# A graph convolution on one core: longer rows of edges with the self-loops squeezed out on chip, and all gathers given to GpSimd

## The reference

```
h = relu(layernorm(x))
out = h @ W_root + bias
for r in range(8):
    m = (edge_type == r)
    msg = h[src] @ W[r] * m
    agg = segment_sum(msg, dst);  cnt = segment_sum(m, dst)
    out += agg / max(cnt, 1)
return x + out
```

## Time and profile before

| | |
|---|---|
| runs shown | 1020.2, 1021.49, 1022.13 us; median 1021.49 us |
| profiled execution | span 1020.0 us from the first to the last instruction |
| busy | PE 769.5 us, DVE 706.0, ACT 413.9, POOL 757.4 |
| GpSimd gathers | 771 from the table and 24 from x |

### The profile page before, as it was taken

One profiled execution on the slowest core, in us unless ns is written; L12 is line 12 of the kernel. 1 busy time (PEld: TensorE's weight loads), 2 busy tenths in 40 slices (PEclk: granted clock), 3 DMA queues, 4 the chain that ended last, 5 costly groups with the idle time before them and its releaser, 6 DMA issues.

```text
span 1020.0 us, 17379 instructions
## 1 busy us (share of the span) xinstructions
PE 769.5 (75%) x4342; PEld 634.1 (62%) x4342; DVE 706.0 (69%) x2309; ACT 413.9 (41%) x821; POOL 757.4 (74%) x808
## 2 busy tenths in 40 slices
PE   0488786887888777877877868878778687787787
PEld 0277675675666665655756756657657566675676
DVE  7798978768776767576666566665765756657676
ACT  7985253352343342432432423423424334243242
POOL 7677777777777777777777777777777777777772
PEclk9996767667676776676676676676766867667679
DMA  9694222222222222222222222222222222222221
GB/s 275 185 226 92 55 58 55 57 57 55 57 56 58 58 58 58 55 59 58 57 56 58 58 55 60 56 58 59 55 59 57 56 60 56 57 58 56 59 57 29
DMA packets 53978, 71.57 MB, mean 70 GB/s; under 512 B 15523, under 2 KB 39110, under 8 KB 53878
## 3 DMA queue, kind: packets, MB, share of 16 engines
q0 software_dynamic: 25440, 52.15, 20.2%
q1 hardware_dynamic: 28438, 18.30, 7.0%
HBM read 63.99 MB, written 6.40 MB: 69 GB/s over the span
## 4 chain that ended last, share of the span: by engine, by line
POOL 52%; issue 19%; PE 14%; DVE 6%; DMA 4%; ACT 4%; SPq 1%; DVEq 0%; POOLq 0%
POOL hg L540 52%; PE acc L1560 5%; PE fin L1591 4%; DMA hg<-h_table,src_i 4%; PE zp L1580 1%; ACT h_all L611 1%; DVE x_all L1146 1%; PE zp L1598 1%; DVE onehot L1048 1%; ACT hg L639 1%; PE acc L1567 1%; PE acc L1564 1%; DMA x_all<-in_x 1%; PE zp L1597 1%; DVE ring L1062 1%
## 5 line engine op out<-in xcount | busy, mean ns | idle before, releaser
L540 POOL DMA_INDIRECT hg<-h_table,src_i x771 | 732.6, 950 | 237.2 <-issue 229.2
L1560 PE MATMUL acc<-onehot,hg 128*128 128x96 f32 (+1 forms) x1602 | 408.3, 367 | 200.7 <-DMA hg<-h_table,src_i 168.4
L1560 PEld LDWEIGHTS acc<-onehot,hg 128*128 128x128 f32 x1602 | 320.9, 249 | 278.6 <-issue 207.1
L1062 DVE TENSOR_TENSOR ring<-ring,acc 128x512 f32 x267 | 181.8, 681 | 239.2 <-PE acc L1567 229.5
L663 ACT ACTIVATE hT<-zp 128x116 f32<-128x116 f32 x50 | 13.4, 267 | 516.3 <-PE zp L1598 516.0
L1048 DVE TENSOR_SCALAR onehot<-iota,key_f 128x96 f32<-128x96 f32 (+1 forms) x801 | 197.2, 293 | 11.4 <-issue 2.6
L1564 PE MATMUL acc<-onehot,ones_bf 128*128 128x96 bf16 (+1 forms) x801 | 204.0, 255 | 0.0
L1591 PE MATMUL fin<-w_sb,blk 128*116 128x128 f32 x800 | 179.3, 398 | 0.0
L1591 PEld LDWEIGHTS fin<-w_sb,blk 128*116 128x116 f32 x800 | 161.6, 288 | 11.9 <-issue 11.7
L653 ACT ACTIVATE loop_far<-iota,loop_key 96x256 f32<-96x256 f32 x267 | 134.0, 502 | 40.9 <-PE acc L1567 28.7
L1146 DVE SCALAR_TENSOR_TENSOR x_all<-fin,inv,x_all 116x128 f32<-116x128 f32 x400 | 139.1, 348 | 14.4 <-DVE x_all L1136 0.5
(11 more groups left out here) (152 smaller groups left out, 369.1 us busy)
## 6 DMA issues: line engine op xcount, KB each, us to landing
hg<-h_table,src_i POOLq DMA_INDIRECT x771, 2.5
hg<-h_table SPq DMA_DIRECT2D x768, 0.5 KB
out<-x_all SPq DMA_DIRECT2D x53, 58.0 KB
x_all<-in_x SPq DMA_DIRECT2D x7, 384.0 KB, 7.9
h_table<-h_all SPq DMA_DIRECT2D x7, 384.0 KB
h_all<-h_table SPq DMA_DIRECT2D x5, 504.0 KB
x_all<-in_x SPq DMA_DIRECT2D x5, 504.0 KB
w_sb<-in_L_gnn_W SPq DMA_DIRECT2D x1, 512.0 KB
```

What stands on the lines that cost most here:

```text
L540: nc.gpsimd.indirect_dma_start(out=hg[:, slot_of(t), :], out_offset=None, in_=x if g < XG else table, in_offset=bass.IndirectOffsetOnAxis( ...
L1062: nc.vector.tensor_tensor(ring[:, :, :, at], ring[:, :, :, at], acc[:, q, :, :].rearrange("p a (r n) -> p a r n", r=R), ALU.add).then_inc( ...
L1560: nc.tensor.matmul(both[:, 0, :, a:e], hg[:, slot, :], hot.rearrange("p (r n) -> p r n", r=R), start=(j == 0), stop=(j == n - 1), skip_gro ...
```

## The change

- Edge rows have three lengths now. The first 126 rows are as before (48 of 128, 78 of 133 edges). Then come 42 rows of 403 edges, each three tiles (384) and 19 spare (`LONG_A`), and 90 rows of 809 edges, each six tiles (768) and 41 spare (`LONG_B`; the last row has 805). A longer row is sure of more self-loops, so 792 tiles hold all edges: 264 groups in place of 267.
- The loops are squeezed out: every edge of a long row gets the number of loops before it, and is moved left by that number in 5 or 6 steps, one per bit (`move(bit)`): a shift-and-mask and a `copy_predicated` over the whole row. This work (`long_steps`) is spread by `long_work` over slots q = 1 to 3 of iterations 3 to 6 (`LONG_A`) and 8 to 11 (`LONG_B`), five steps an iteration. It replaces `run_ends` to `loop_tops` of parts 1 to 3.
- The edge rows are loaded by five DMAs per array again (`edge_rows`), in the same places of SyncE's queue: 48, 78, 42, 89 and 1 rows.
- `FETCHED` is empty: SyncE fetches no rows, GpSimd gathers all 264 groups (792 gathers).
- Groups are numbered from slot 3 of iteration 0 (`G0` = 3), so blocks meet the same slots of iterations as before; group g is where group g + 3 was, EARLY is 257 and ENDG 262. The windows of long rows' one-hots are 12 or 13, 14 and 16 nodes wide (before 12, 12 and 17).
- Sources of part 1 are ready after slot 3 of iteration 7 (group 35, needed at group 42), those of part 2 after iteration 13 (group 65, needed at 84).

```diff
-FETCHED = (209, 264)
+FETCHED = ()
+LONG_A = Long(42, 3, 19, 5, (138,), RC, FIRST_EDGES, 1)
+LONG_B = Long(90, 6, 41, 6, (138, 542), RC + LONG_A.rows * LONG_A.tiles, ...)
+G0 = VGROUPS - GALL
-            def chunks(a, v):
-                w, done = RAW + (a == 1), edges_in[a]
-                sp.dma_start(e_rows_i[0:WHOLE, a, 0, 0:w], rows_of(v, 0, WHOLE, None, w, P)).then_inc(done, 16)
-                sp.dma_start(e_rows_i[WHOLE:RC, a, 0, 0:w], rows_of(v, WHOLE, RC - WHOLE, None, w)).then_inc(done, 16)
-                sp.dma_start(e_rows_i[:, a, 1:CHUNKS - 1, 0:w], rows_of(v, RC, RC, CHUNKS - 2, w)).then_inc(done, 16)
-                sp.dma_start(e_rows_i[0:ROWS_L - 1, a, CHUNKS - 1, 0:w],
-                             rows_of(v, RC * (CHUNKS - 1), ROWS_L - 1, None, w)).then_inc(done, 16)
...
+            def edge_rows(a, v):
+                more, done = a == 1, edges_in[a]
+                w = RAW + more
+                sp.dma_start(first_i[0:WHOLE, a, 0:w], rows_of(v, 0, WHOLE, w, P)).then_inc(done, 16)
+                sp.dma_start(first_i[WHOLE:RC, a, 0:w], rows_of(v, WHOLE * P, RC - WHOLE, w, RAW)).then_inc(done, 16)
+                w = LONG_A.width + more
+                sp.dma_start(long_i[0][:, a, 0:w], rows_of(v, LONG_A.first_edge, LONG_A.rows, w, LONG_A.width)).then_inc(done, 16)
+                w, rows = LONG_B.width + more, LONG_B.rows - 1
+                sp.dma_start(long_i[1][0:rows, a, 0:w], rows_of(v, LONG_B.first_edge, rows, w, LONG_B.width)).then_inc(done, 16)
...
-                    nc.vector.tensor_copy(e_rows[:, 1, :, :], e_rows_i[:, 1, :, :]).then_inc(dst_conv, 1)
+                    for to, of in zip([first, *long], [first_i, *long_i]):
+                        nc.vector.tensor_copy(to[:, 1, :], of[:, 1, :]).then_inc(dst_conv, 1)
...
+            def long_steps(k):
...
+                def run_ends_of_long():
+                    counted(nc.vector.tensor_tensor(one, d, long[k][:, 1, 1:w + 1], ALU.subtract))
+                    counted(nc.vector.tensor_copy(srcs, word_i))
+                def keys_of_long():
+                    counted(nc.vector.tensor_tensor(keys, d, keys, ALU.add))
+                    checked(nc.vector.tensor_tensor(two, srcs, d, ALU.subtract))
+                def differ():
+                    checked(nc.vector.tensor_tensor(two, two, one, ALU.mult))
...
+                def loop_values():
+                    counted(nc.vector.scalar_tensor_tensor(out=two, in0=keys, scalar=ABOVE, in1=one, ...))
...
+                def loops_before():
+                    counted(nc.vector.tensor_scalar(two, d, d[:, 0:1], None, ALU.subtract))
+                    counted(nc.vector.scalar_tensor_tensor(out=two_i, in0=one, scalar=1.0, in1=two, ...))
+                def whole_words():
+                    counted(nc.vector.scalar_tensor_tensor(out=word_i, in0=keys, ..., in1=srcs, ...))
+                def shifts_into_words():
+                    counted(nc.vector.tensor_scalar(two_i, two_i, SHIFT_AT, None, ALU.logical_shift_left))
+                    counted(nc.vector.tensor_tensor(word_i, word_i, two_i, ALU.bitwise_or))
+                def move(bit):
+                    def step():
+                        by = 1 << bit
+                        counted(nc.vector.tensor_scalar(one_i[:, by:], word_i[:, by:], SHIFT_AT + bit, 1, ...))
+                        counted(nc.vector.copy_predicated(word_i[:, 0:w - by], one_i[:, by:], word_i[:, by:]))
...
+            def long_work(i, q):
+                for k, since in enumerate(LONG_FROM):
+                    at = 5 * (i - since) + (0, 0, 1, 3, 5)[q]
+                    if since <= i and 1 <= q <= 3:
+                        for step in long_steps(k)[at:at + (0, 1, 2, 2, 0)[q]]:
+                            step()
```

More of the change, by code:

```diff
@@ L167, in rgcn @@
[L167 to L170, removed]
+        first_i = sb("first_rows", [RC, 3, RAW + 1], i32)
+        long_i = [sb(f"long_rows{k}", [v.rows, 3, v.width + 1], i32) for k, v in enumerate(LONGS)]
+        first = first_i[:, :, :].bitcast(f32)
+        long = [v[:, :, :].bitcast(f32) for v in long_i]
+        scratch = sb("scratch", [P, 2, LONG_B.width + 1])
@@ new lines, in rgcn @@
+        long_node = sb("long_node", [LONG_B.rows, LONG_B.tiles, 2])
+        long_gap = sb("long_gap", [LONG_B.rows, LONG_B.tiles + 5])
+        long_bad = sb("long_bad", [LONG_B.rows, 4 * LONG_B.tiles + 8])
+        apart = sb("apart", [P, LONG_B.rows])
+        heads = sb("heads", [RC, GALL])
+        lead = sb("lead", [RC, RG, GT])
+        in_rows = lambda k, n: scratch[0:RC, 0, k * RAW:k * RAW + n]
+        ends, near_key, loop_val, loop_rest, rank, words = (in_rows(k, RAW) for k in range(6))
@@ L327, in from_x, with event_at, tiles_of, words_of @@
         def from_x(i, q):
[L329 to L336, removed]
+            return i * GROUPS + q - G0 < XG
+        def event_at(i, q, step_q, when):
+            return when.index(i) if q == step_q and i in when else None
+        def tiles_of(v, e):
+            part, half = WORDS[e]
+            if part == 0:
+                return v[:, 0:RC]
+            long_of = LONGS[part - 1]
+            at = long_of.first_tile
+            return v[:, at:at + long_of.rows * long_of.tiles].rearrange("e (p m) -> e p m", m=long_of.tiles)[
+                :, :, half * GT:(half + 1) * GT]
+        def words_of(v, e):
+            part = WORDS[e][0]
+            if part == 0:
+                return v[:, 0:RC]
+            return v[:, 0:LONGS[part - 1].rows * GT].rearrange("e (p j) -> e p j", j=GT)
         def terms_before(b):
@@ L685, in iteration @@
                         tile_h(g)
-                    if static(i) and q == 1:
-                        for c in range(1, CHUNKS):
-                            typed_offsets(c)
+                    if g == 1:
+                        for part in range(1, len(PART_GROUPS)):
+                            typed_offsets(part)
                     if static(i, 1) and q == 3:
@@ L1511, in word_transposes @@
-            def word_transposes(part):
-                c0, n = PARTS[part]
-                pe.wait_ge(words_full, part + 1)
-                for k in range(n):
-                    last = nc.tensor.transpose(wordsT[:, k * RC:(k + 1) * RC], words[:, k, 0:P], ident[0:RC, 0:RC])
+            nc.tensor.matmul(baseT[:, 0:RG], ones[0:RC, :], heads[:, 0:RG], start=True, stop=True).then_inc(base_T, 1)
+            for v in LONGS:
+                at = slice(v.first_group, v.first_group + v.rows * v.groups)
+                nc.tensor.matmul(baseT[:, at], ones[0:v.rows, :], heads[0:v.rows, at], start=True, stop=True).then_inc(base_T, 1)
@@ new lines, in word_transposes @@
+            def word_transposes(e):
+                part, half = WORDS[e]
+                pe.wait_ge(words_full, part + 1)
+                if part == 0:
+                    nc.tensor.transpose(wordsT[:, 0:RC], words[:, 0:P], ident[0:RC, 0:RC]).then_inc(words_T, 1)
+                    return
+                n = LONGS[part - 1].rows
+                for j in range(GT):
+                    at = (half * GT + j) * P
+                    last = nc.tensor.transpose(wordsT[:, j * n:(j + 1) * n], long[part - 1][:, 2, at:at + P], ident[0:n, 0:n])
```

788 lines of the change are left out of this document (468 added, 320 removed).

## The result

The changed kernel takes 1046.86 us (median of 4 runs, 1046.03 to 1047.01); the kernel before took 1021.81 beside it (4 runs, 1020.2 to 1023.44). The ratio is 1.0244, 95% interval 1.0229 to 1.0258: 25 us slower. The profiled execution has a span of 1044.0 us. (In two of the four comparisons further down, those whose kernel before is at 1244.7 and at 1234.22 us, every kernel took 1216 us or more, with engines standing still where no engine and no DMA in the trace released them, so each time is set only against its own comparison's kernel before.)

A forecast was written before the change was run, and what follows sets the result against it. Bound: start until `h_stored` (35.5), GpSimd's paced gathers up to group 259, and an end of 41.5 us. Sum 1020.0 - 7.5 + 4 + 28.5 = 1045.0 profiled, 1046 as median; range 1022 to 1066.

The forecast's parts named there:

- 1. Gathers removed: GpSimd's gathers up to old group 259: six fewer at 1.247 us, -7.5 us; three more in the end part hidden.
- 2. VectorE's long instructions: Gathers beginning inside long VectorE instructions, mainly two-input ones, take longer: +4 us, ends -2.3 and +14.7.
- The factor of 1.5: Gather lengthening counted in the old trace (2.3 us) over the formula's 1.5 us; raised the new estimate from 5.6 to 8.4.
- the formula: Average gather delay per VectorE instruction with data part d: d x d / (2 x 1.247); 5.6 us together after the change.
- 3. VectorE's extra work: Iterations 8 to 11: VectorE falls behind by up to 5 us, covered by slots ten groups deep: 0.
- 4. The edge loads: Start: one DMA engine carries each array's 89-row piece, stores of h queue behind; `h_stored` at 64, not 35.5: +28.5 us.
- rival D: Edge loads: SyncE also stands still with other engines idle, or unaligned reads run at half rate: above 1066; chance 0.05.
- rival B: Edge loads: a different single engine for each piece, running side by side; `h_stored` 6 late, 1024; chance 0.08.
- 5. Small things: Casts of dst and heads on VectorE, and windows of 42 or 43 nodes on TensorE: 0.
- A (rows spread after all): Edge loads: 89-row piece cut other than by whole rows, `h_stored` stays near 35.5, 1018; chance 0.08.
- C (VectorE as the bound): `h_stored` little late, but VectorE's waits and slower predicated copies exceed the slots' cover: 1028 to 1033; chance 0.04.

The follow-up runs named there:

- the split kernels: Changed kernel with each edge array's 89-row piece loaded as 80 and 9 rows, also with further additions; split alone 1021.13 us, ratio 0.9981 to the kernel before.
- the maxima: Kernel with 89-row loads cut in 80 and 9, plus 60 unused VectorE row maxima of 90 x 809 elements in iterations 20 to 39: 1019.39 us.
- the sixty sums: Kernel with 89-row loads cut in 80 and 9, plus 60 unused two-input VectorE sums of 90 x 809 elements in iterations 20 to 39: 1036.16 us.
- The version with groups 206 and 261: Kernel with 89-row loads cut in 80 and 9, SyncE again fetching these two groups' source rows: ratio to the kernel before 1.0112, then 0.9933 (1015.48 us).

## Why the prediction was right, step by step

**What bounds it.** It is bounded as predicted: start until `h_stored`, gathers at a pace, an end of 41.5 us: the account above closes to a tenth with these three parts, and in the split kernels the end was 41.5 to 42.1.

**1. Gathers removed, -7.5.** As predicted, six gathers of 1.247. The three more in the end part were covered (41.3 against 41.5).

**2. VectorE's long instructions, +4.** Measured +4.2 over the 746 steps. The largest delay is a two-input instruction of 809 elements. Timeline of VectorE and GpSimd in the changed kernel:

```profile
187.45 1.00 DVE L1084 TENSOR_TENSOR scratch<-scratch 90x809 f32<-90x809 f32 x1
187.51 1.76 POOL L612 DMA_INDIRECT hg<-h_table,src_i  x1 [0.30 <-issue]
...
189.79 3.68 DVE L1058 TENSOR_REDUCE ext<-scratch 90x1 f32<-90x809 f32 x4
190.82 0.95 POOL L612 DMA_INDIRECT hg<-h_table,src_i  x1 [0.30 <-issue]
192.08 0.94 POOL L612 DMA_INDIRECT hg<-h_table,src_i  x1 [0.30 <-issue]
```

The reductions, beside which gathers keep their 0.94, weren't counted, rightly. `copy_predicated`, which had no row, was priced about right: 1.03 to 1.12 us for `LONG_B`, and six gathers that began inside one took 2.3 us longer in sum. The size of the whole, though, has luck in it: the same instructions cost more in the split kernels. The split kernel's steps are 1.2642 in one run; with the maxima, which cost next to nothing, 1.2615. That is 5.9 to 7.9 us over the 1.2536 of before, inside the predicted -2.3 to +14.7 but above its +4. In the run with 1.2642 about 3 us of it is that all gathers were slower (a mean of 950 ns from 320 to 975 us, where `LONG_B` is done, against 946 before); why, no run shows. So the split's profile is only 0.8 us shorter than before: -7.5 for the gathers, +7.9 for the steps, -1.8 for an earlier first gather, +0.6 at the end; the medians are 2.2 apart, and 3.3 were expected. The factor of 1.5 has no support from the sixty sums, where the formula alone was right (16.8 against 16.6); it gave half of what one-input instructions cost, 4 for 9.0. The Trainium skill (SBUF — State Buffer, Who interferes with whom) has whoever comes second blocked until the other is through; the rows agree but for the last eighth of a microsecond, 0.56 us where 0.68 were left.

**3. VectorE's extra work, 0.** Right: "PE acc L1816: 4.9, 16, 0.3" is all that GpSimd waited for slots, and 60 instructions of 1 us more, the maxima, didn't show in the time either (one run).

**4. The edge loads, +28.5.** Measured 27.5, `h_stored` at 63.3 for 64. Shown by the two experiments on both sides: divisible rows in the changed kernel take the delay away, a prime number of rows in the kernel before brings one of 36.3 us. src's arrival (55.19, predicted 53 to 56) and the waits for x's third and fifth steps are as predicted. Two things went otherwise than I wrote. SyncE itself also stands at the instruction behind the second and the third piece, which rival D named. The sum of what one engine has to carry came out even so; that the standing costs nothing more, since what SyncE would issue needs that engine too, is argued and not shown. And ScalarE isn't done before the third piece lets the stores through: it needed 14.2 us for its last columns (41.6 to 55.85), not some 12, and ended 0.7 us after src had landed, so the last stores waited for it. The time is the sum's even so: after src's 55.19 us the engine has its sixteenth of h left, 200 KB, 8.2 us at the prediction's faster rate of 24.5 GB/s, which gives 63.4. The chain over ScalarE alone would have given 59.2. With a few us more on ScalarE the step would have come out too short, so here too there is some luck. The Trainium skill (DMA: Bandwidth & Descriptors, Why a DMA increments its semaphore by 16 and not by 1) puts the divisor on the slowest dimension; 113 x 5 rows going to one engine agrees. Which engine it is, no run shows. That the three pieces follow each other on the same one fits the arrivals at 22.55, 39.62 and 55.19 us; with another engine for each (rival B) they would have run side by side, and h would have been stored at 42 us.

**5. Small things.** Nothing of them is visible in the end part (41.3 us, before 41.5).

**The rivals.** A (rows spread after all) and B (another engine each time) were ruled out by the first gather at 63.31 us. C (VectorE as the bound) was tested apart from the late start by the split kernel: no wait for a slot over 0.5 us. Of D one condition came true, SyncE standing still while the other engines idle, but not its time, above 1066 us.

## What to carry to other kernels

Check the number of partition rows of every DMA for its largest divisor up to 16: three loads of 89 rows cost 27.5 us at the start and three of 113 x 5 cost 36.3, and 80 + 9 costs nothing measurable. Treat such a load as an obstacle in the queue, not as a slow transfer: what is issued behind it lands late, and behind a second one it isn't even issued. Then look at what waits for the transfers held up: here x's late steps alone would have made the stores of h 23.4 us late, by the estimate above. Where GpSimd's gathers set the pace, six gathers less are 7.5 us only if the VectorE work that is bought with them isn't made of full-width instructions; count those, and leave reductions out.

## What was not expected of the hardware

- SyncE stood for 11.0 and 7.1 us at one instruction right behind an 89-row load and took 6.6 us over the five loads of x after the first of these, and it took 14.7, 18.0 and 16.3 us over the loads of 565 and 65 rows, the first of which is on one engine. The whole core showed 19 GB/s at a share of 0.08 with rows of 0.53 KB, and 24 to 34 at 0.06 to 0.09 with rows of 3.2 KB and more under way.
- Sixty `tensor_scalar` on 90 x 809 elements lengthened the gathers that began inside them by 9.0 us, about 0.15 us each; sixty `tensor_reduce` over as many elements, 0.3 us in all.
- Fetching 32 rows one by one with SyncE took 14.3 us beside a kernel before of 1022.52 us, and over 30 us beside one of 1234.22. The version with groups 206 and 261 gained 0.7% against the kernel before of 1022.52 us and lost 1.1% against that of 1244.7.
